# Constants, zeros, a load and du(2) moved in unit 0, and the order of the end, in a Mamba and mixture-of-experts kernel

## The reference, cut to what matters

```python
h = layer_slice[input_ids]                               # (2, 2048, 64)
# attn(u): layernorm, in_w, causal conv of 4 taps, silu -> act; per direction:
x = silu(conv(x)); x_dbl = x @ xproj_w.T
dt = softplus(x_dbl[..., :R] @ dt_w.T + dt_b)
h_t = h_{t-1} * exp(dt * A) + (dt * x) * B               # scan over time, 16 states
y = (h_t * C).sum(states) + x * D
out = y * silu(z) @ out_w.T                              # then gate, out_w, residual
h = h + attn(layernorm(h))
# ffn(u): idx = argmax(u @ router_w.T + router_b); relu(relu(u W1[idx] + b1) W2[idx] + b2)
h = h + ffn(layernorm(h))
```

## Time and profile before

| | |
|---|---|
| median of 3 runs | 562.32 us (561.82 to 569.52) |
| the profiled execution | 559.91 us |
| its span, first to last instruction | 558.1 us |
| VectorE busy | 489.1 us (88%) |
| GpSimd busy | 474.9 us (85%) |
| TensorE busy | 457.3 us (82%) |
| ScalarE busy | 372.6 us (67%) |
| mean granted TensorE clock | 0.934 of full speed |

### The profile page before, as it was taken

One profiled execution on the slowest core, in us unless ns is written; L12 is line 12 of the kernel. 1 busy time (PEld: TensorE's weight loads), 2 busy tenths in 40 slices (PEclk: granted clock), 3 DMA queues, 4 the chain that ended last, 5 costly groups with the idle time before them and its releaser, 6 DMA issues.

```text
span 558.1 us, 5617 instructions
## 1 busy us (share of the span) xinstructions
PE 457.3 (82%) x1621; PEld 175.5 (31%) x1621; DVE 489.1 (88%) x606; ACT 372.6 (67%) x651; POOL 474.9 (85%) x157
## 2 busy tenths in 40 slices
PE   2976977868889797979798889888988895785877
PEld 1422422313233231424232423232324232332243
DVE  3575895989899999999999899999998999999940
ACT  2488485686877776776968497869684974564433
POOL 5552877998989989899999999999999999989700
PEclk9998998999989897989999799999997997697998
DMA  4249397949293855738493949493939392900000
GB/s 58 18 63 218 77 218 149 217 114 207 76 199 88 182 124 134 173 87 175 115 181 117 200 115 190 119 197 105 201 109 208 98 208 86 222 13 1 5 5 19
DMA packets 51008, 71.05 MB, mean 127 GB/s; under 512 B 16498, under 2 KB 17442, under 8 KB 50978
## 3 DMA queue, kind: packets, MB, share of 16 engines
q1 hardware_dynamic: 47986, 69.36, 55.0%
q0 software_dynamic: 1024, 1.05, 2.4%
q10 hardware_dynamic: 1968, 0.29, 0.3%
HBM read 60.19 MB, written 10.49 MB: 127 GB/s over the span
## 4 chain that ended last, share of the span: by engine, by line
DVE 45%; PE 24%; issue 11%; ACT 9%; POOL 6%; DMA 3%; SPq 2%; POOLq 0%; DVEq 0%; ACTq 0%
DVE st L1504 26%; DVE st L1489 8%; POOL st L491 4%; PE ps L727 3%; ACT ps L1081 2%; PE ps L628 2%; PE ps L690 2%; PE ps L703 2%; PE ps L817 2%; PE ps L715 2%; DVE zr L1510 1%; PE ps L801 1%; ACT L979 1%; PE ps L698 1%; DVE ga L1516 1%
## 5 line engine op out<-in xcount | busy, mean ns | idle before, releaser
L491 POOL TENSOR_TENSOR st<-st,repC 128x2048 f32<-128x2048 f32 x63 | 285.2, 4530 | 18.1 <-ACT carry L1087 13.0
L1504 DVE TENSOR_TENSOR_SCAN st<-ps,carry,st 128x512 f32<-128x512 f32 x192 | 235.5, 1268 | 3.7 <-ACT ps L1081 3.1
L1081 ACT ACTIVATE ps<-dtS,negA 128x512 f32<-128x512 f32 x256 | 171.2, 682 | 63.1 <-DVE st L1504 61.8
L482 POOL TENSOR_TENSOR st<-duS,repB 128x2048 f32<-128x2048 f32 x30 | 135.9, 4530 | 1.7 <-issue 1.7
L1504 DVE TENSOR_TENSOR_SCAN st<-ps,zero,st 128x512 f32<-128x512 f32 x64 | 78.9, 1270 | 1.4 <-ACT ps L1081 1.0
L715 PE MATMUL ps<-st,fold 128*32 128x512 f32 x504 | 69.0, 620 | 12.8 <-POOL st L491 12.8
L1489 DVE TENSOR_TENSOR st<-duS,ps 128x2048 f32<-128x2048 f32 x33 | 75.0, 2272 | 1.9 <-PE ps L690 1.7
L628 PE MATMUL ps<-act,wT 128*128 128x512 f32 x128 | 57.8, 593 | 0.3 <-ACT act L1025 0.3
L463 POOL DMA_INDIRECT x<-in_L_tok_ple_table,idx x32 | 31.1, 973 | 29.6 <-DMA dtS<-dt_dram 13.4
L690 PE MATMUL ps<-xr,Bw 128*128 128x512 f32 x68 | 38.2, 645 | 6.2 <-ACT bc_sb L1073 6.2
L667 PE MATMUL ps<-xr,wT 128*32 128x512 f32 x32 | 18.1, 649 | 26.3 <-DVE st L1489 26.3
(11 more groups left out here) (138 smaller groups left out, 622.2 us busy)
## 6 DMA issues: line engine op xcount, KB each, us to landing
repC<-bc_dram SPq DMA_DIRECT2D x64, 256.0 KB, 10.5
duS<-du_dram SPq DMA_DIRECT2D x60, 256.0 KB, 4.7
dtS<-dt_dram SPq DMA_DIRECT2D x60, 256.0 KB, 7.8
repB<-bc_dram SPq DMA_DIRECT2D x60, 128.0 KB, 2.9
dt_dram<-dt SPq DMA_DIRECT2D x16, 256.0 KB, 3.0
du_dram<-du SPq DMA_DIRECT2D x16, 256.0 KB, 2.0
bc_dram<-bc_sb SPq DMA_DIRECT2D x16, 64.0 KB, 11.1
dtS<-dt_dram SPq DMA_DIRECT2D x8, 128.0 KB, 3.4
```

The costliest lines, as they stand in the source:

```text
L482: pool.tensor_tensor(st[:, r], duS[:, u % 2], row, ALU.mult).then_inc(sem("dbu_pool"), 1)
L491: pool.tensor_tensor(st[:, r], st[:, r], row, ALU.mult).then_inc(sem("hc_ready"), 1)
L1081: sc.activation(decay_bank(u, r, q), dtS[:, u % 2, q], ACT.Exp, scale=negA[:, way(u), q, r:r + 1]).then_inc(sem("decay_ready"), 1)
L1504: dve.tensor_tensor_scan(st[:, r, q, order], decay_bank(u, r, q)[:, order], st[:, r, q, order], first, ALU.mult, ALU.add).then_inc(sem("sc ...
```

## The change

It moves steps within the lists of the engines, adds one wait, and adds one multiplication with zeros at the end.

- SyncE: in unit 0 the load of B for unit 1 stands ahead of the stores of dt and du of unit 1.
- GpSimd: dt(1) times x stands ahead of the first C product of unit 0; the last four gathers stand behind the third C product of unit 0; dt(2) times x stands in unit 1 behind the last C product of unit 0. From unit 1 on the order is as before.
- TensorE: in the opening, skip and the three multiplications with zeros stand ahead of `turn_chunk(3)`, which waits for VectorE. At the end, `logits(before)` stands ahead of the third partial sum in place of the fourth; `hidden(before, 3)` stands ahead of `turn_normed(last)`, with one multiplication with zeros behind the latter.
- ScalarE: `dt_out(u)` also waits until the product du of unit u-1 has been made; the relu of `hidden(before, 3)` stands ahead of `normed_out(last)`.
- VectorE: the copies of `rank` and of the mask stand at the end of the opening; at the end `by_gate(last)` stands ahead of `choice(before)`.

```diff
@@ -417,10 +417,10 @@
                 first_half(h)
             load_C(0)
             store_bc(1)
+            load_B(1)
             store_dt(1)
             store_du(1)
             load_du(1)
-            load_B(1)
             load_dt(1)
             load_C(1)
             with nc.allow_non_contiguous_dma(reason="b1 is 2 KB"):
@@ -511,22 +511,24 @@
             for u in range(UNITS):
                 if u:
                     by_c(u - 1, NR - 1)
+                if u == 1:
+                    dt_times_x(2)
                 if u == 0:
                     pool.wait_ge(sem("dt_first_1"), 64)
                     for t in range(TB + 4, TB + 12):
                         gather(t)
+                    dt_times_x(1)
                 if 2 in on_pool(u):
                     input_product(u, 2)
                 by_c(u, 0)
-                if u == 0:
-                    dt_times_x(1)
-                    for t in range(TB + 12, TILES):
-                        gather(t)
                 by_c(u, 1)
                 if u + 1 < UNITS:
                     input_product(u + 1, 0)
                 by_c(u, 2)
-                if u + 2 < UNITS:
+                if u == 0:
+                    for t in range(TB + 12, TILES):
+                        gather(t)
+                if 0 < u < UNITS - 2:
                     dt_times_x(u + 2)
             u = UNITS - 1
             for q in range(NQ - 1):
@@ -845,9 +847,9 @@
             conv(1, 2)
             pre(1)
             bc(1)
-            turn_chunk(3)
             skip_product(0)
             add_nought(3)
+            turn_chunk(3)
             b_rows(0, 1)
             sum_dt(1)
             x_chunk(2, LONG)
@@ -948,10 +950,11 @@
             sum_states(last, 2)
             turn_normed(before)
             for q in range(NQ):
+                if q == 2:
+                    logits(before)
                 if q < NQ - 1:
                     pe.wait_ge(sem("hc_ready"), NR * UNITS + q)
                 else:
-                    logits(before)
                     pe.wait_ge(sem("hc_dve"), 1)
                 mm = pe.matmul(ps[32 * q:32 * q + 32, Y, :], fold[:], st[:, NR - 1, q],
                                start=False, stop=True, skip_group_check=True)
@@ -962,8 +965,9 @@
             hidden(before, 0)
             hidden(before, 1)
             hidden(before, 2)
+            hidden(before, 3)
             turn_normed(last)
-            hidden(before, 3)
+            add_nought(1, start=True)
             logits(last)
             experts_out(before)
             turn_choice(last)
@@ -1065,6 +1069,7 @@
             def dt_out(u):
                 sc.wait_ge(sem("dt_ps"), u)
                 wait(sc, "dt_in_dram", 16 * u)
+                sc.wait_ge(sem("du_ready"), u)
                 sc.activation(dt[:], ps[:, PRE, :], ACT.Copy).then_inc(sem("dt_ready"), 1)
 
             def bc_out(u):
@@ -1317,8 +1322,8 @@
             hidden_relu(before, 1)
             rsqrt(NCH + nth(last))
             hidden_relu(before, 2)
+            hidden_relu(before, 3)
             normed_out(last)
-            hidden_relu(before, 3)
             moe_relu(before)
             choice_mask(last)
             hidden_relu(last, 0)
@@ -1479,6 +1484,10 @@
             begin_norm(3)
             norm_var(3)
             rates(1)
+            dve.wait_ge(sem("consts"), 1)
+            ch.mark(dve.tensor_copy(rank[:], ranki[:]))
+            ch.mark(dve.tensor_copy(w1[DM:DM + E], maskf))
+            ch.wait()
 
             def input_product(u, r):
                 if u:
@@ -1656,11 +1665,6 @@
                     start_residual(3)
                 if p == 3:
                     input_product(0, 1)
-                if p == 4:
-                    dve.wait_ge(sem("consts"), 1)
-                    ch.mark(dve.tensor_copy(rank[:], ranki[:]))
-                    ch.mark(dve.tensor_copy(w1[DM:DM + E], maskf))
-                    ch.wait()
                 if p == 5:
                     input_product(0, 2)
                 if p == 8:
@@ -1685,8 +1689,8 @@
             y_by_z(last)
             best_expert(before)
             first_best()
+            by_gate(last)
             choice(before)
-            by_gate(last)
             add_partial(last)
             norm_first(NCH + nth(last), x0_of(tile0(last)))
             norm_centre(NCH + nth(last), x0_of(tile0(last)))
```

## The result

The kernel takes 555.53 us after the change (median of 17 runs, 551.94 to 562.6) against 560.34 us before (17 runs, 556.29 to 569.52). The ratio is 0.9914, with a 95% interval of 0.9893 to 0.9935: 4.8 us less, between 3.6 and 6.0. By the bound of 2% this is no change; against the runs' own scatter it is clearly faster. The profiled execution has a span of 552.7 us, 5.4 us less than before.

A forecast was written before the change was run, and what follows sets the result against it. VectorE was taken to set the pace of the steady part, which the change leaves alone. Opening -2.6 and end -1.3 gave -3.9 us, from the median of 562.32 to 558.4; range 555.0 to 562.0.

The forecast's parts named there:

- The copies cost nothing in the opening: End of the opening: VectorE waits 3.98 us there anyway, so the moved copies cost nothing, at most 3.1 us.
- the cast was held by GpSimd: Unit 0, between two scans: the cast's 2.67 us are a standstill until GpSimd is done, not its own work.
- TensorE's chain sets the gain, the rest becomes a wait before scan 12: Unit 0: TensorE's chain gives 2.6 us, VectorE's could give 4.9; about 2.5 us wait for ScalarE before scan 12.
- The clock during the sum of dt(1): TensorE, unit 0: clock falls some 2 us before the sum, back near 58.2; gain 2.6 us, ends 1.0 and 3.5.
- rival 1: The clock stays up over the opening: 3.5 us gained there, 557.5 in all; chance 0.14.
- GpSimd keeps its place at the seam: Seam to unit 1: GpSimd's input product (1,2) starts at 93.2, not 97.06, gaining 3.9 us where the others gain 2.6.
- wait of 1.71 us for the row of B: GpSimd's input product of unit 1 waited 1.71 us, thought for its row of B, whose load now stands earlier.
- The term of the partial sums: End, TensorE: logits ahead of the third partial sum use the wait for GpSimd, about 0.2 us gained.
- The exchange of choice and gate: End, VectorE: by_gate ahead of choice costs 0.4 us, since TensorE's order is unchanged.
- The clock in the experts' output: End, TensorE: one more full pair may hold the clock; the sixteen matmuls then take 1.95 us, 1.6 less.
- Rivals 3: The change does nothing to speak of: wins waited off by unit 1, end pays 0.2 us; 562.5, chance 0.11.
- rival 4: Slower: GpSimd becomes the bound at the seam if the third C product starts later than about 80; 564.6, chance 0.07.

The follow-up runs named there:

- experiments 1: Kernel before with only the two copies of constants moved to the opening: ratio 0.9984 (0.9948 to 1.0021).
- experiment 2: Kernel before with only skip and the zeros put ahead of the fourth transpose: ratio 1.0000 (0.9958 to 1.0042).
- experiment 5: Kernel before with all edits of the end and none of the opening: ratio 0.9961 (0.9932 to 0.9990), 2.2 us less.
- experiment 3: Kernel before with both copies and zeros moved, nothing else: ratio 0.9955 (0.9928 to 0.9981), 2.5 us less.
- experiment 4: Kernel before with all edits of the opening and unit 0, end as before, timed twice: ratio 0.9991, then 0.9962.
- experiment 10: Kernel before with only copies, zeros, logits, and hidden(3) with the end's zeros changed: ratio 0.9903 (0.9872 to 0.9934), median 555.00 us.
- experiment 6: Kernel before with only logits ahead of the third partial sum; one execution: last scan pair to product with z 4.83 us in place of 6.05.
- experiment 8: Kernel after with choice(before) again ahead of by_gate(last) on VectorE: ratio to before 0.9924 (0.9895 to 0.9952).
- experiment 7: Kernel before with only hidden(3) ahead of the last norm's transposes and zeros in its place; one execution: product with z to end 24.27 us.

## Why the prediction was right, point by point

- **Time and bound.** Forecast from its own basis 3.9 us less, measured 4.8 (3.6 to 6.0). The median after is 555.53, inside 555.0 to 562.0 but near its lower end. The median of before was 562.32 in three runs and is 560.34 in 17. So 2 us of the forecast's 558.4 were the three runs, and the change was worth 1 us more than forecast. The range is no test by itself: 560.34, the time without the change, lies in it too. What bears the forecast out are the stretches.
- **The copies cost nothing in the opening, and the cast was held by GpSimd.** Right, shown by experiments 1 and 2. It isn't always held by both products (experiment 5).
- **TensorE's chain sets the gain, the rest becomes a wait before scan 12.** Right: 1.67 us there after the change. I had about 2.5 us, and had named 2 us as the sign; it is less by what TensorE gained more than forecast (next point).
- **The clock during the sum of dt(1).** Here the size was off. The forecast took a fall some 2 us ahead of the sum, and 2.6 us of gain. After the change the clock stayed up and scan 0 to scan 12 shrank by 3.57 us, which is rival 1's 3.5 us. It stayed up in all six further executions that were profiled with the opening whole or the four edits. In experiments 2 and 3 it fell at 54.5 and 54.6, as forecast, and experiment 3 then gained 2.8 us. So both cases exist; the price of the fall is 0.76 us (27.45 against 26.69), and it may strike in other runs of the change too. The forecast also took the clock of the one trace of before (down from 51.3 to 58.2) as given. In the four traces with the old opening the stretch took 28.56 to 30.30 us (experiment 4), so part of the 3.57 us is luck of that trace, and 3.1 is the better figure. What the zeros in the gap do is clearer: without them the clock fell in five of five traces between 50.1 and 54.0, in or just behind TensorE's gap of 3.0 to 4.2 us ahead of the transposes; with them it fell in two of nine. By chance such a split comes in about 1 of 100. The rule of the Trainium skill, "TensorE: Matmul & The Clock Gate", section "HAM oscillation — how this bites in real kernels", on long gaps, gave the case that came more often. The fall at 54.5 in experiment 2, behind gaps of 0.8 and 1.7 us, speaks against it as the only cause.
- **GpSimd keeps its place at the seam.** Right: input product (1,2) began at 94.16, 2.9 us earlier than before, although scan 0 was 2.0 us later. I had 93.2. Experiment 10 adds that the whole reordering of GpSimd and the load of B could have been left out. The wait of 1.71 us for the row of B went, as I had it, and nobody gained by it. What the new order of the loads did take away is a wait of ScalarE for dt (experiment 10), which the forecast doesn't have.
- **The end.** The term of the partial sums was mis-sized: forecast 0.2 us, measured 1.2 us (experiment 6). I had counted only the wait for GpSimd, and not that the last two sums run side by side once nothing stands between them. The exchange of choice and gate was forecast at 0.4 us of loss and cost 0.31 (experiment 8). The clock in the experts' output held, and the sixteen matmuls took 1.95 us as forecast, but it held in three of seven executions without the edit too (experiment 7), so that it was up in this one is in part luck. Some 0.9 of the 1.6 us is the change's on average, if the new order always keeps it up.
- **Sum of the mis-sizings.** From 3.9 us: opening 0.5 us more (3.1 in the mean), partial sums 1.0 us more, clock at the end some 0.7 us less in the mean: 4.7 us, against 4.8 measured. With means of four to seven traces the closeness is partly chance.
- **Rivals 3 and 4** (nothing, or GpSimd the bound) didn't occur. For rival 4 the third C product would have had to start later than 80; it started at 79.06 in a trace that was 2 us late from its start.

## What to carry to other kernels

When two engines alternate on a path, an edit on one of them shows nothing until the other's is made too: 0.4 us and a loss alone, 2.8 us together. A small copy or cast on VectorE that falls beside long GpSimd products may last until the product, or both of two, have ended (1.23 to 4.58 us in place of 0.17), so such copies belong where GpSimd is idle. Two sums that go to different column strips should stand next to each other in TensorE's list. And one trace of before is a weak yardstick: the same stretch, unchanged, took 28.56 to 30.30 us in four.

## What the runs showed of the hardware that I had not expected

The stretch from scan 17 to the last scan is the same code in every kernel here. Yet it took 429.4 to 434.0 us in 14 profiled executions. What differs between them in the traces is how long and where TensorE's granted clock fell to half: it was down for 37.5 us in the fastest and 68.3 us in one of the two slowest. But nine traces with 61.4 us each range from 431.4 to 434.0 us, so the length alone isn't the whole cause, and no run isolates it. The times show the same. Of 64 executions of the kernel before, timed with the experiments, 11 have a mean granted clock of at least 0.952 and took 555.9 to 557.9 us (median 556.1); the other 53 have at most 0.937 and took 558.8 to 565.2 (median 561.0). After the change, 4 of 17 have at least 0.956 (median 554.1 us) and 13 at most 0.938 (median 556.4). The profiled execution of after is one of the first kind, that of before (0.934) one of the second. Within a kind the change gives 2.1 and 4.6 us; these runs weren't timed together, and four are few, but it fits that a part of the gain is time at the lower clock that is avoided.

A spread of 4.6 us in unchanged code is about that of one kernel's own times, and as large as the effect of this change. The opening showed the same: the taps of the first chunk took 1.99 us in the trace of before and 3.4 in that of after, from identical lists. In a kernel like this, edits of 1 us are read from stretches of the trace between two scans, not from the times, and from more than one trace of each.
